# Routed blocks of 256 rows in place of pairs of 128-row tiles, in a transformer with routed experts

## The chip, the cores and the metric

The kernel runs on one core of a Trainium2 chip. The core has TensorE (PE in the profile, its weight loads PEld), VectorE (DVE), ScalarE (ACT), GpSimd (POOL) and SyncE (SP, which here only issues DMAs), SBUF as working memory and PSUM as the place where TensorE writes. The metric is the device time of one execution in microseconds: 3275.05 us, the median of 3 runs (3268.84 to 3275.7).

## The reference, cut to what matters

Sixteen sequences of 256 rows of 128 numbers pass a prologue (layer norm, a small wavelet network with linear attention) and then four layers of this:

```python
for l in range(4):
    h = rms(x, ln1_w[l])
    q, k, v = h @ wq[l], h @ wk[l], h @ wv[l]       # 16 query heads, 4 key/value heads of 64
    x = clip(x + attention(rope(q), rope(k), v, causal) @ wo[l], -100, 100)
    h = rms(x, ln2_w[l])
    probs = softmax(h @ wr[l])                      # 8 experts
    topv, topi = top_k(probs, 2)
    topv = topv / topv.sum(-1, keepdims=True)
    out = 0
    for e in range(8):                              # only rows that chose e count
        g = silu(h @ wg[l, e]) * (h @ wu[l, e])     # 128 -> 256
        out += comb[..., e:e+1] * (g @ wd[l, e])    # 256 -> 128
    x = clip(x + out, -100, 100)
```

Each row goes to two of eight experts. The kernel computes only those two per row.

## The kernel before

**The main loop.** `for it in range(-1, NIT + 1)` runs over 64 pairs of layer and sequence, and each engine has its own copy of this loop, written out by hand. One pass for `it` holds attention of sequence `it` (four groups `q` of four heads: `scores`, `mask_and_max`, `exps`, `normalise`, `attend`), the projections of `it + 1` (`project_qk`, `rope`) and output projection and routing of `it - 1` (`project_out`, `update_x`, `choose`, `route`). Each engine executes its instructions in order, and semaphores say when data or a PSUM bank is ready.

**The routed work.** `route` gives each row a slot in a region of its expert in HBM, and POOL sends the rows there by an indirect DMA (`scatter`, L1299). Eight sequences make a batch. When a batch is routed, `lay_out_tiles` (DVE) makes a table of tiles, 128 rows of one expert each; 40 tiles hold any distribution (32 full ones and up to 8 that are partly empty), and 40 are always computed, as 20 pairs. A pair takes two half-steps. In the even one `turn_rows` transposes 2 x 128 rows on PE (L891), `round_rows` (ACT, L1133) and `low_rows` (DVE, L1683) split them into a rounded part and a rest, and the pair before has its 4 gated blocks transposed (`turn_gated`, L912) and split (`round_gated` L1142, `low_gated` L1694). In the odd one `gate_and_up` multiplies each tile by its expert's weights, 3 products of 512 columns per tile (L902 to L904), ACT takes a tanh (`open_gate`, L1138), DVE two products (`gate`, L1689 and L1690), and the pair before goes through `down` (12 products of 128 columns, L926 to L928) and `copy_y` (ACT, L1147). SP fetches rows and weights and puts results back, two tiles separately: 8 DMAs a pair, each with a register load from the table (`tile_place`, L567).

**Where the half-steps stand.** A pass of the loop has eight places, 0 to 7, between its pieces. A batch's 42 half-steps are put in the next batch's passes: four in the second pass (places 4 to 7), all eight in the third to sixth, six in the seventh. The first and the eighth pass have none. I call a pass with all eight a dense pass: 4 pairs. The last batch has no later pass: its 42 half-steps run after the loop, the tail, with `finish` of the first eight sequences between them. Results come back by indirect DMAs (`gather`, L1275, in the loop and L1362 at the end).

**PSUM.** Eight banks form three rings. S (4 banks, freed by DVE): scores, q/k projections, output projection. T (2 banks, freed by ACT): transposed probabilities, v, h, logits, ranks, and y of the routed work. U (2 banks, freed by DVE): attention output, transposed rows, gates, transposed gated blocks. A tenant of a ring waits until the one that stood there before has been read.

## Time and profile before

| | |
|---|---|
| median of 3 runs | 3275.05 us |
| profiled execution, its own time | 3285.71 us |
| its span, first to last instruction | 3283.9 us |
| PE / PEld busy | 2618.0 us (80%) / 2095.5 us (64%) |
| DVE / ACT / POOL busy | 2207.6 (67%) / 1996.6 (61%) / 1861.3 us (57%) |
| granted TensorE clock, mean | 0.919 |
| DMA moved | 511.54 MB, of it 473.72 MB by SP's queue |

Busy shares are means over a prologue (to about 245 us), the loop (to about 3060 us) and the tail. A PE that is 80% busy is not at 80% of its peak: a matmul's time in the profile overlaps the next one's. For PE the distance between the starts of two neighbours says what one costs.

### The profile page before, as it was taken

The numbers are of one execution on the slowest core, as the hardware profiler recorded it, in microseconds if no ns is written. First come the engines' busy times: TensorE is split into PE (matmuls) and PEld (weight loads), VectorE is DVE, ScalarE is ACT, GpSimd is POOL, SyncE is SP. The second block draws the span as 40 slices with busy tenths as digits, with TensorE's granted clock in tenths as the row PEclk, the third lists the DMA queues.
The fourth block names the chain that finished last, engine by engine and source line by source line (L and its number), as shares of the span: only waits on it lengthen the run. The fifth ranks groups of instructions, "written<-read, shape, count | busy, mean of one in ns | idle before, by whom it ended". The sixth has DMA issues, their size and how long they took to land.

```text
span 3283.9 us, 66162 instructions
## 1 busy us (share of the span) xinstructions
PE 2618.0 (80%) x20406; PEld 2095.5 (64%) x20406; DVE 2207.6 (67%) x8164; ACT 1996.6 (61%) x7080; POOL 1861.3 (57%) x1662
## 2 busy tenths in 40 slices
PE   5317887898889987899789987898889978998572
PEld 2316666777667766777667766777677766776462
DVE  6686676666777667776676767677676666765343
ACT  3017677667667666666666766676666766666220
POOL 0026676545666667655765666566766576555403
PEclk9659999999999999999999999999999999999665
DMA  9211122556246642654256633654266624652574
GB/s 373 118 46 65 68 78 86 181 177 198 71 161 212 206 137 80 222 192 154 77 189 228 212 106 116 201 194 139 74 214 218 200 76 145 201 193 89 164 240 128
DMA packets 287022, 511.54 MB, mean 156 GB/s; under 512 B 39969, under 2 KB 159297, under 8 KB 286145
## 3 DMA queue, kind: packets, MB, share of 16 engines
q1 hardware_dynamic: 270288, 473.72, 42.6%
q0 software_dynamic: 16384, 33.59, 3.3%
q8 instruction: 167, 2.74, 0.4%
q14 instruction: 183, 1.49, 0.2%
HBM read 316.58 MB, written 106.69 MB: 129 GB/s over the span
## 4 chain that ended last, share of the span: by engine, by line
PE 43%; DVE 19%; ACT 12%; POOL 11%; issue 7%; SPq 3%; another core or an unknown queue 3%; DMA 2%; DVEq 0%; POOLq 0%
PE psum L784 6%; PE psum L802 6%; DVE arena L1572 5%; ACT arena L1055 4%; PE psum L759 4%; PE psum L852 4%; POOL arena L1308 4%; ACT arena L1063 3%; PE psum L804 3%; POOL arena L1275 2%; DVE arena L1593 2%; PE psum L902 2%; PE psum L832 2%; POOL rows_in L1299 2%
## 5 line engine op out<-in xcount | busy, mean ns | idle before, releaser
L1055 ACT ACTIVATE arena<-arena 128x128 f32<-128x128 f32 (+1 forms) x2048 | 902.3, 446 | 53.4 <-DVE arena L1597 47.5
L1308 POOL TENSOR_TENSOR arena<-arena 128x512 f32<-128x512 f32 (+1 forms) x512 | 743.6, 1472 | 208.4 <-DVE arena L1602 208.3
L1323 POOL TENSOR_TENSOR arena<-arena 128x512 f32<-128x512 f32 x320 | 401.6, 1282 | 491.6 <-DMA arena<-arena 491.3
L784 PE MATMUL psum<-arena 128*128 128x128 f32 x3072 | 478.1, 294 | 225.5 <-ACT arena L1063 154.9
L1063 ACT COPY arena<-psum 128x384 f32<-128x384 f32 x1024 | 447.5, 482 | 312.7 <-PE psum L784 217.4
L784 PEld LDWEIGHTS psum<-arena 128*128 128x128 f32 x3072 | 347.5, 147 | 341.0 <-ACT arena L1063 214.5
L759 PE MATMUL psum<-arena 64*128 64x128 f32 (+1 forms) x4096 | 419.8, 342 | 12.7 <-DVE arena L1593 7.0
L1593 DVE CUSTOM_DVE_ANT_0 arena<-psum,arena 128x256 f32<-128x256 f32 x1024 | 429.3, 419 | 0.0
L1606 DVE COPY arena<-psum 128x512 f32<-128x512 f32 x256 | 176.4, 689 | 347.3 <-PE psum L804 314.2
L1572 DVE TENSOR_TENSOR arena<-psum,arena 128x512 f32<-128x512 f32 x640 | 390.8, 675 | 1.9 <-PE psum L834 1.8
L1055 ACT ACTIVATION_READ_ACCUMULATOR arena<-arena 128x1 f32 x2048 | 389.9, 190 | 0.0
L802 PE MATMUL psum<-arena 128*64 128x256 f32 x2048 | 355.3, 428 | 35.7 <-DVE xT_lo L1683 30.2
L759 PEld LDWEIGHTS psum<-arena 64*128 64x128 f32 x4096 | 301.3, 190 | 55.7 <-issue 26.2
L1591 DVE CUSTOM_DVE_ANT_0 arena<-psum,arena 128x128 f32<-128x128 f32 x1024 | 292.4, 286 | 31.3 <-PE psum L759 17.0
L1299 POOL DMA_INDIRECT rows_in<-arena x256 | 259.4, 1013 | 75.3 <-issue 69.3
L852 PE MATMUL psum<-arena 128*128 128x128 f32 x2048 | 247.3, 279 | 27.6 <-issue 27.5
L852 PEld LDWEIGHTS psum<-arena 128*128 128x128 f32 x2048 | 240.3, 196 | 37.0 <-issue 36.5
L832 PE MATMUL psum<-h_hi,wqk_hi 128*128 128x256 f32 x640 | 197.1, 308 | 69.2 <-DVE arena L1593 52.6
L804 PEld LDWEIGHTS psum<-arena 128*64 128x64 f32 x2048 | 160.3, 150 | 91.6 <-issue 26.7
L1275 POOL DMA_INDIRECT arena<-rows_out,arena x192 | 189.1, 985 | 52.3 <-issue 52.3
L804 PE MATMUL psum<-arena 128*64 128x128 f32 x2048 | 215.1, 290 | 0.0
L1689 DVE SCALAR_TENSOR_TENSOR arena<-arena,psum 128x512 f32<-128x512 f32 x160 | 108.0, 675 | 149.2 <-ACT arena L1138 122.9
(199 smaller groups left out, 5440.5 us busy)
## 6 DMA issues: line engine op xcount, KB each, us to landing
gu<-gu_kept SPq DMA_DIRECT2D x320, 512.0 KB
wd<-wd_kept SPq DMA_DIRECT2D x320, 256.0 KB
arena<-arena SPq DMA_DIRECT2D x128, 384.0 KB, 3.0
arena<-arena SPq DMA_DIRECT2D x128, 256.0 KB
arena<-rows_in SPq DMA_DIRECT2D x320, 64.0 KB
rows_out<-arena SPq DMA_DIRECT2D x320, 64.0 KB
rows_in<-arena SPq DMA_DIRECT2D x34, 512.0 KB, 8.0
rows_out<-arena SPq DMA_DIRECT2D x34, 512.0 KB, 7.1
```

The source lines that it names most:

```text
L759: return T.matmul(psum[:, s_bank(("head", it, q, i)), cols], QKT[par][r, 2 + 2 * q + i // 2, rows * P:(rows + 1) * P], QKT[par][r, q // 2, ...
L784: mm = T.transpose(psum[:, t_bank(key), j * P:(j + 1) * P], probs[:, q, i, j * P:(j + 1) * P], ident)
L802: return T.matmul(psum[r, bank, c0:c0 + S], v[:, 0, kv], pt[:, 0:S], start=True, stop=False, skip_group_check=True)
L804: return T.matmul(psum[r, bank, c0 + P:c0 + S], v[:, 1, kv], pt[:, S:S + P], start=False, stop=True, skip_group_check=True)
L852: mm = T.matmul(psum[:, s_bank(("out", it)), t * P:(t + 1) * P], oT[:, c, t * P:(t + 1) * P], wo[:, c, :], start=(c == 0), stop=(c == NH / ...
L1055: ins = A.activation(a, a, ACT.Exp, bias=negmax[:, q, k:k + 1], accum_out=rowsum[:, q, k:k + 1])
L1063: A.copy(probsT[:, 4 * (q % 2) + i, :], psum[:, t_bank(key), 0:3 * P]).then_inc(sem("t_free"), 1)
L1299: G.indirect_dma_start(rows_in[b % 2], bass.IndirectOffsetOnAxis(place_of[:, it % B * ST + t, j:j + 1], 0), z2[:, it % 2, t, :], None).the ...
L1308: ins = G.tensor_tensor(a, a, r[:, :, t:t + 1].broadcast_to([P, 4, P * (t + 1)]), ALU.mult)
L1323: G.tensor_tensor(keys_and_queries(it, u), keys_and_queries(it, u), turned_part[:, u, :], ALU.add) \
L1572: return V.tensor_tensor(dst.rearrange("p (i s) -> p i s", i=2), psum[:, s_bank(("qk", it, u)), :].rearrange("p (i s) -> p i s", i=2), tab ...
L1593: V.tensor_tensor_reduce(probs[:, q, i, P:3 * P], psum[:, s_bank(key), P:3 * P], mask, SCALE, -3.0e38, ALU.add, ALU.max, rowmax[:, q, 2 * ...
```

## The change

**Blocks.** A unit of work is 256 rows of one expert instead of two tiles of 128. A batch of eight sequences needs 23 units for any distribution (16 + 7), one of four 15. Both halves of a unit use the same weights, so one fetch of 768 KB (`w_kept`, rounded part and rest of all three matrices) replaces two of 512 KB and two of 256 KB, and a unit has 3 DMAs instead of 8.

**Gates come out transposed.** `gate_and_up` has the weights as the stationary side and the rows as the moving one: 12 products of 256 columns instead of 6 of 512. Their result is already turned as `down` wants it, so `turn_gated` is gone, and `round_gated` and `low_gated` read SBUF.

**Rings.** Transposed rows move from the U ring to the T ring. ACT now writes them twice (rounded and exact), and DVE forms the rest from SBUF. Gates of units that run beside no scores (the last pass and the tail, the set `late`) use the S ring.

**Places.** A step is now `gate_and_up` of one unit, `turn_rows` of the next, `down` of the one before. A batch has 25 steps: places 5 and 7 of the second pass, places 1, 2, 3, 5, 7 of the third to sixth, 1, 2, 3 of the seventh. On ACT `round_gated` and on DVE `low_rows` and `low_gated` stand at the place's end, after the piece that follows.

**Batches.** The last batch of eight is cut in two of four. The first of these (15 units, 17 steps) stands at places 5 and 7 of the pass for `it` 62, 1 to 7 of 63 and 0 to 7 of 64; the second is the tail, with a third pair of HBM buffers.

```diff
-NB = NIT // HB
+FIRST = [HB * b for b in range(NIT // HB)] + [NIT - 4]
+END = FIRST[1:] + [NIT]
+NB = len(FIRST)
 CAP = HB * S
-PT = 20
-HS = 2 * PT + 2
-ROWS = NE * CAP + NE * P
+UR = 2 * P
+UNITS = [2 * (b - a) + NE - 1 for a, b in zip(FIRST, END)]
+UNIT0 = [sum(UNITS[:b]) for b in range(NB + 1)]
+ROWS = NE * CAP + NE * UR
...
+def step_places():
+    at = {}
+    for b in range(NB - 1):
+        last = END[b] - 1
+        if b < NB - 2:
+            places = [(last + 1 + u, p) for u, ps in ((1, (5, 7)), (2, (1, 2, 3, 5, 7)), (3, (1, 2, 3, 5, 7)),
+                                                      (4, (1, 2, 3, 5, 7)), (5, (1, 2, 3, 5, 7)), (6, (1, 2, 3))) for p in ps]
+        else:
+            places = [(NIT - 2, 5), (NIT - 2, 7)] + [(NIT - 1, p) for p in range(1, 8)] + [(NIT, p) for p in range(8)]
+        for k, where in enumerate(places):
+            at[where] = (b, k)
+    return at
...
+    def moe(b, k):
+        g = UNIT0[b] + k
+        if 1 <= k <= UNITS[b]:
+            ring = s if g - 1 in late else u
+            ring["gate", g - 1] = len(ring)
+            ring["up", g - 1] = len(ring)
+        if k < UNITS[b]:
+            t["rows", g] = len(t)
+        if k >= 2:
+            t["y", g - 2] = len(t)
...
+            def fetch(b, k):
+                g = UNIT0[b] + k
...
+                if g >= X_RING:
+                    t_is_full(sp, ("rows", g - X_RING))
+                if g >= W_RING:
+                    t_is_full(sp, ("y", g - W_RING))
+                sp.load([row_reg[g % ROW_REGS], expert_reg], tiles[k:k + 1, b % 2, :])
+                sp.dma_start(x_rows[:, g % X_RING, :, :], rows_in[buffer_of(b)][unit_rows(g), :].rearrange("(j p) c -> p j c", p=P)) \
+                    .then_inc(sem(f"x_rows_in{g % X_RING}"), 16)
...
+                sp.dma_start(w_now[:, g % W_RING, :, :].rearrange("p k n -> p (k n)").bitcast(F32), w_kept[which, :]) \
+                    .then_inc(sem(f"w_in{g % W_RING}"), 16)
...
+            def after_step(b, k):
+                if k >= 2:
+                    put_back(b, k - 2)
+                if 2 <= k < UNITS[b] - 2:
+                    fetch(b, k + 2)
+                if k == UNITS[b] + 1 and b == NB - 3:
+                    begin(b + 1)
...
             def gate_and_up(g):
-                pe.wait_ge(sem(f"gu_in{g % W_RING}"), 32 * (g // W_RING + 1))
-                u_was_read(pe, ("rows", g))
-                for j in range(2):
-                    key = ("gate", g, j)
-                    u_is_free(key)
-                    o = psum[:, u_bank(key), :]
-                    hi, lo = (a[:, j * P:(j + 1) * P] for a in (xT_hi, xT_lo))
-                    T.matmul(o, hi, gu[:, g % W_RING, j, 0:2 * FF], start=True, stop=False)
-                    T.matmul(o, hi, gu[:, g % W_RING, j, 2 * FF:4 * FF], start=False, stop=False)
-                    T.matmul(o, lo, gu[:, g % W_RING, j, 0:2 * FF], start=False, stop=True).then_inc(sem("u_full"), 1)
+                pe.wait_ge(sem(f"w_in{g % W_RING}"), 16 * (g // W_RING + 1))
+                pe.wait_ge(sem("xT_lo_ready"), g + 1)
+                hi, lo = (a[:, g % 2, :] for a in (xT_hi, xT_lo))
+                for m, name in enumerate(("gate", "up")):
+                    gate_is_free(name, g)
                     for f in range(2):
+                        o = psum[:, gate_bank(name, g), f * UR:(f + 1) * UR]
+                        w_h, w_l = (w_now[:, g % W_RING, k, (2 * m + f) * P:(2 * m + f + 1) * P] for k in range(2))
+                        T.matmul(o, w_h, hi, start=True, stop=False)
+                        T.matmul(o, w_h, lo, start=False, stop=False)
+                        mm = T.matmul(o, w_l, hi, start=False, stop=True)
+                    mm.then_inc(gate_full(g), 1)
...
+            def step_of(b, k):          # TensorE
+                g = UNIT0[b] + k
+                if 1 <= k <= UNITS[b]:
+                    gate_and_up(g - 1)
+                if k < UNITS[b]:
+                    turn_rows(g)
+                if k >= 2:
+                    down(g - 2)
...
             def round_rows(g):
-                u_is_full(act, ("rows", g))
-                A.mul(xT_hi, psum[:, u_bank(("rows", g)), 0:2 * P], lnw[:, 1, l:l + 1]).then_inc(sem("xT_hi_ready"), 1)
+                t_is_full(act, ("rows", g))
+                rows = psum[:, t_bank(("rows", g)), 0:UR]
+                A.mul(xT_hi[:, g % 2, :], rows, lnw[:, 1, l:l + 1])
+                A.mul(xT[:, g % 2, :], rows, lnw[:, 1, l:l + 1]).then_inc(sem("t_free"), 1)
...
             def round_gated(g):
-                u_is_full(act, ("gated", g))
-                A.copy(hh_hi, psum[:, u_bank(("gated", g)), :]).then_inc(sem("hh_hi_ready"), 1)
+                gate_was_read(act, "up", g)
+                A.copy(hh_hi, gated).then_inc(sem("hh_hi_ready"), 1)
...
             def low_gated(g):
                 dve.wait_ge(sem("hh_hi_ready"), g + 1)
-                V.tensor_tensor(hh_lo, psum[:, u_bank(("gated", g)), :], hh_hi.bitcast(F32), ALU.subtract) \
-                    .then_inc(sem("u_free"), 1)
+                V.tensor_tensor(hh_lo, gated, hh_hi.bitcast(F32), ALU.subtract).then_inc(sem("hh_lo_ready"), 1)
...
-            for hs in range(HS):
-                moe(NB - 1, hs)
-                if hs % 4 == 3 and hs // 4 < HB:
-                    finish(hs // 4)
+            for k in range(UNITS[-1] + 2):
+                step_of(NB - 1, k)
+                step_end(NB - 1, k)
+                if k % 2 == 0 and 1 <= k // 2 <= HB:
+                    finish(k // 2 - 1)
```

The order of instructions moves on every engine. TensorE at place 2 of a dense pass, before: `project_v` (L841), the rows and gated blocks turned (L891, L912), `project_out` (L852).

```order
L841 MATMUL psum<-arena 128x256 [waits t_free,wv_in]
L841 MATMUL psum<-arena 128x256
L891 MATMUL psum<-arena 128x128 [waits u_free,x_rows_in1]
L891 MATMUL psum<-arena 128x128
L912 MATMUL psum<-arena 128x128 [waits u_free]
L912 MATMUL psum<-arena 128x128 x3
L852 MATMUL psum<-arena 128x128 [waits s_free,u_free,wo_in]
```

The same place now: `project_v` (L861), `gate_and_up` (L929 to L931), `turn_rows` (L911), `down` (L942 to L944), `project_out` (L872).

```order
L861 MATMUL psum<-arena 128x256
L929 MATMUL psum<-xT_hi,w_now 128x256 [waits u_free,xT_lo_ready,w_in0]
L930 MATMUL psum<-xT_lo,w_now 128x256
L931 MATMUL psum<-xT_hi,w_now 128x256
...
L929 MATMUL psum<-xT_hi,w_now 128x256 [waits u_free]
...
L911 MATMUL psum<-arena 128x128 [waits t_free,x_rows_in1]
L911 MATMUL psum<-arena 128x128
L942 MATMUL psum<-w_now,hh_hi 128x128 [waits t_free,hh_lo_ready]
...
L872 MATMUL psum<-arena 128x128 [waits s_free,u_free,wo_in]
```

Six transposes ahead of `project_out` have become a whole step of 26 products, and two of its waits are now for the T ring, whose tenants here run v, rows, y.

ScalarE at place 1 of a dense pass, before: tanh (L1138), `copy_y` (L1147), the copies of probabilities (L1063), squares of the coming sequence (L1077).

```order
L1138 ACTIVATE arena<-psum 128x512 [waits u_full]
L1147 ACTIVATE arena<-psum 128x256 [waits y_rows_out0,t_full]
L1063 COPY arena<-psum 128x384 [waits t_full] x4
L1077 ACTIVATE arena<-arena 128x128 [waits x_ready]
L1077 ACTIVATE arena<-arena 128x128
```

The same place now: tanh (L1154), rows rounded and copied (L1149, L1150), `copy_y` (L1164), the probabilities (L1074), `round_gated` (L1159), the squares (L1088).

```order
L1154 ACTIVATE arena<-psum 128x512 [waits u_full]
L1149 ACTIVATE xT_hi<-psum,arena 128x256 [waits t_full]
L1150 ACTIVATE arena<-psum,arena 128x256
L1164 ACTIVATE arena<-psum 128x256 [waits y_rows_out0,t_full]
L1074 COPY arena<-psum 128x384 [waits t_full] x4
L1159 CAST hh_hi<-arena 128x512 [waits u_free]
L1088 ACTIVATE arena<-arena 128x128 [waits x_ready]
L1088 ACTIVATE arena<-arena 128x128
```

Two instructions at this place have become five, one of them behind the probabilities and ahead of the squares.

## Rows read from the trace of the kernel before

**Rows 1.** The page's chain of waits that ended last, shares of the span by engine.

```profile
PE 43%; DVE 19%; ACT 12%; POOL 11%; issue 7%; SPq 3%; another core or an unknown queue 3%; DMA 2%; DVEq 0%; POOLq 0%
```

**Rows 2.** Stretches: us, busy PE, PEld, DVE, ACT, POOL, PEclk, DMA share, GB/s.

```profile
1337.00:1525.00 188.00, 171.55 (x1400) 140.56 (x1396) 133.20 (x516) 129.40 (x458) 111.44 (x100) 0.99 0.60 200
3043.00:3067.00 24.00, 9.55 (x83) 7.62 (x79) 6.97 (x38) 4.14 (x14) 9.84 (x12) 0.78 0.06 23
3067.00:3236.00 169.00, 117.70 (x480) 97.57 (x480) 67.78 (x136) 40.29 (x80) 29.71 (x32) 0.63 0.72 231
```

**Rows 3.** L1612, once a pass: count, first and last start, in three windows.

```profile
L1612 DVE TENSOR_TENSOR arena<-arena,psum x5: 420/421/422, 368.2 to 512.7; 128x256 f32<-128x256 f32 x5
...
L1612 DVE TENSOR_TENSOR arena<-arena,psum x4: 410/410/420, 1357.6 to 1499.4; 128x256 f32<-128x256 f32 x4
...
L1612 DVE TENSOR_TENSOR arena<-arena,psum x9: 410/420/422, 1357.6 to 1713.8; 128x256 f32<-128x256 f32 x9
```

**Rows 4.** Instructions by line in the four dense passes: busy, mean ns, idle before.

```profile
L802 PE MATMUL psum<-arena 128*64 128x256 f32 x128 | 21.1, 408 | 5.4 <-DVE xT_lo L1683 4.1 <-ACT arena L1063 1.2
...
L1694 DVE TENSOR_TENSOR hh_lo<-psum,hh_hi 128x512 fp32r<-128x512 f32 x16 | 10.9, 681 | 0.0
L1689 DVE SCALAR_TENSOR_TENSOR arena<-arena,psum 128x512 f32<-128x512 f32 x16 | 10.8, 672 | 9.1 <-ACT arena L1138 7.7 <-issue 1.4
...
L1138 ACT ACTIVATE arena<-psum 128x512 f32<-128x512 f32 x16 | 9.4, 585 | 6.3 <-PE psum L904 6.3
L1142 ACT CAST hh_hi<-psum 128x512 fp32r<-128x512 f32 x16 | 9.3, 584 | 0.0
...
L1133 ACT ACTIVATE xT_hi<-psum,arena 128x256 fp32r<-128x256 f32 x16 | 7.5, 472 | 4.5 <-PE psum L891 4.5
...
L1683 DVE SCALAR_TENSOR_TENSOR xT_lo<-psum,arena,xT_hi 128x256 fp32r<-128x256 f32 x16 | 7.3, 454 | 14.3 <-ACT xT_hi L1133 14.3
...
L1147 ACT ACTIVATE arena<-psum 128x256 f32<-128x256 f32 x16 | 6.0, 375 | 1.6 <-PE psum L928 1.4 <-issue 0.2
```

**Rows 5.** Timeline of PE in one dense pass: start us, us, what.

```profile
1399.71 0.38 PE L891 MATMUL psum<-arena 128*128 128x128 f32 x2
...
1400.37 3.74 PE L852 MATMUL psum<-arena 128*128 128x128 f32 x32
...
1405.82 0.50 PE L902 MATMUL psum<-gu,xT_hi 128*128 128x512 f32 x1
...
1407.31 0.22 PE L926 MATMUL psum<-wd,hh_hi 128*128 128x128 f32 x1
...
1408.60 0.33 PE L832 MATMUL psum<-h_hi,wqk_hi 128*128 128x256 f32 x1
...
1410.08 0.38 PE L861 MATMUL psum<-arena 128*128 128x128 f32 x2
```

**Rows 6.** Timeline of DVE and of ACT, same pass.

```profile
1398.86 0.69 DVE L1606 COPY arena<-psum 128x512 f32<-128x512 f32 x1 [1.56 <-PE psum L804]
...
1401.88 0.56 ACT L1067 COPY arena<-psum 128x512 f32<-128x512 f32 x1
```

**Rows 7.** Timeline of PE in the tail.

```profile
3075.26 0.80 PE L902 MATMUL psum<-gu,xT_hi 128*128 128x512 f32 x1 [1.29 <-DMA gu<-gu_kept]
...
3137.54 0.76 PE L902 MATMUL psum<-gu,xT_hi 128*128 128x512 f32 x1 [1.30 <-issue]
...
3142.72 0.66 PE L891 MATMUL psum<-arena 128*128 128x128 f32 x2
```

**Rows 8.** Chain of waits in the tail: start us, us, what.

```profile
3064.88 2.22 DMA rows_in<-arena
...
3221.62 0.77 PE psum L902
...
3236.11 0.94 POOL arena L1362
...
3275.16 2.54 DMA arena<-rows_out,arena
```

404 lines of the change are left out of this document (185 added, 219 removed).

## The prediction

> **What bounds the kernel now.** I read the page first. Its chain of waits [rows 1] passes through PE for 43% of the span, DVE 19%, ACT 12%, POOL 11%: PE leads, but no engine alone sets the time. Then the spacing of one instruction that stands once in each pass, the add of `update_x` [rows 3]. Without routed work (368.2 to 512.7, four distances) a pass takes 36.1 us, a dense one (1357.6 to 1499.4, three distances) 47.3, and eight passes of a batch 356.2 (1357.6 to 1713.8), of which the four that are not dense keep 167.0, or 41.7 each. Four pairs thus add 11.2 us. Third, the stretch of four dense passes [rows 2]: in 188 us PE is busy 171.55, DVE 133.20, ACT 129.40. Per pass PE has 4.1 us without work, ACT 14.7 and DVE 13.7, and the clock is granted at 0.99, the level of 2.4 GHz. The tail is another regime: clock 0.63, mostly at 1.2 GHz, DMA at 231 GB/s, and a pair takes (3221.62 - 3075.26) / 19 = 7.70 us [rows 7, 8].
>
> **The change in a dense pass.** PE's work I take from distances between starts [rows 5]. A pair costs 0.66 for six transposes (1399.71 to 1400.37), 1.49 for two tiles of gates (1405.82 to 1407.31) and 1.29 for `down` (to 1408.60), together 3.44. A unit has 2 of the 6 transposes, 0.22, the same `down`, 1.29, and 12 products of 256 columns. These have the shape of `project_qk`, of which 12 took 1.48 (1408.60 to 1410.08). That makes 2.99. A batch costs PE 20 x 3.44 = 68.8 before and 23 x 2.99 = 68.8 now: the padding of 23 blocks eats exactly what the transposes gave. But the five places put 5 x 2.99 = 14.95 in a dense pass that had 4 x 3.44 = 13.76: +1.2.
>
> ACT [rows 4]: a pair has 0.472 + 0.585 + 0.584 + 0.375 = 2.02, a unit one more copy of the rows (0.472), 2.49. Five against four: 12.4 - 8.1 = +4.4 a pass. DVE: 0.454 + 2 x 0.672 + 0.681 = 2.48 for either (`low_rows` and `low_gated` now read SBUF; I keep their PSUM prices), so +2.5. Both fit in the idle time of 14.7 and 13.7 by sum, not necessarily by place.
>
> `round_gated` reads SBUF instead of PSUM; the nearest row is its present form, 584 ns [rows 4]. The Trainium skill (VectorE: DVE Perf Modes, The TRN2 errata) gives ScalarE a fixed 224 cycles for an SBUF source and 172 for PSUM, at 1.2 GHz, so an estimate from that page is 613 against 570 ns for 512 columns. The trace's 584 is near the second. By the page ACT gets 191 x 0.04 = 8 us more over the kernel, by the row nothing; both are off the path of my sum.
>
> Waits of PE. One goes: attention's second product (L802) waited 4.1 us in four passes for `low_rows` to free a U bank [rows 4], 1.0 a pass. Transposed rows no longer stand in that ring. One comes, at place 2. PE is through with `project_v` at 1399.71 [rows 5]. The gates there want `low_rows` of the step before, which on DVE now stands behind the copy of attention's output (1398.86 + 0.69 = 1399.55 [rows 6]) and takes 0.45: 1400.0, and with a hand-over 1400.1, a wait of 0.4. Gates and transposes take 1.70, so `down` is reached at 1401.8. Its bank in the T ring held v, and v is read at 1401.88 + 0.56 = 1402.44 [rows 6], because on ACT that copy stands behind eight exponentials. Another 0.6. Queued behind `down` is `project_out`, then h, the scores and, through `update_x`, everything of the second half. (v's copy itself moves by -0.66, the transposes gone from place 0, and +0.58, `round_gated` now ahead of the squares: nothing.) So +1.2 - 1.0 + 1.0 = +1.2. I take +1.5, as some of ACT's 4.4 will be in the way. Bounds: all of ACT's extra on the path, +4.4; or eight hand-over points made five take 3/8 of PE's 4.1 idle, -1.5, and the place-2 wait does not come: 1.2 - 1.0 - 1.5 = -1.3.
>
> The other passes have 5 pairs and now 5 units, PE -2.2, against one place-2 wait in the seventh: -1.0 a batch (-2.2 to +2). **Loop:** 7 x (4 x 1.5 - 1.0) = **+35** (-52 to +137).
>
> I give nothing for the weights' traffic, 1.5 MB a pair down to 0.75 a unit. No idle time in rows 4 ends on it; what hides it is the lead of the fetches, and if that were too short the tail would tell first. The prologue zeroes half as many HBM buffers again; by the slices of the page DMA stands still there while VectorE works on the wavelets, so 0.
>
> **Passes 62 to 64.** They take 17 steps of the first half-batch. The pass for 62 goes from three pairs to five units, from 41.7 to 48.8: +7. The one for 63 had nothing and gets 7 units, 20.9 us of PE. At the dense rate (11.2 us for 13.76 of work) that is +17; if they fill all of the 10 us that a light pass leaves PE, +11. It has no projections for a coming sequence, so 12. The last pass, 3043 to 3067, is a chain of latencies with PE busy for 9.55 of 24 us [rows 2]. Eight units are 23.9 us of PE and 14.4 are free: +9.5 at best, +24 at worst; every step also wants its answer from ACT and DVE, so 14. Together **+33** (27 to 48).
>
> **The tail.** Rows have landed at 3064.88 + 2.22 = 3067.10, gates run from 3075.26 to 3221.62, the last results are back when POOL gathers at 3236.11, and 31 distances to 3275.16 make 1.26 us a gather [rows 7, 8]. The span ends at 3283.9, 216.8 us after the rows landed. Now there are 15 units. At the low clock a pair without transposes took 5.18 (3137.54 to 3142.72 [rows 7]) where 1.49 + 1.29 = 2.78 stood in the loop, a factor of 1.86; a unit's 2.99 becomes 5.6. I take 5.7, PE setting the pace. SP's part falls from 8 DMAs to 3, and 1.05 MB in 5.7 us is 184 GB/s, below the 231 reached. So 8.2 to the first gate, 14 x 5.7 = 80 to the last, 14.5 to the gather, and only four sequences wait for it: 47.8 - 16 x 1.26 = 27.6. That is 130: **-87**. Bounds: 14 x 7.70 if the pace stays, -59; 14 x 4.5 if the clock rises and the hand-over loop binds (half of the gates 0.74, tanh 0.59, two products 1.34, `low_rows` 0.45, and `finish` every second step, 1.2), -103.
>
> **Sum:** 35 + 33 - 87 = -19. The profiled execution took 3285.7 (1.8 more than its span), 10.7 above the median of 3275.05, so 3267 for it and **3256** for the median.
>
> **Rivals.**
> *A: fewer hand-overs win.* A dense pass falls by 1.3. For: PE's idle time is made of short waits, and the tenants that blocked attention leave the U ring; DVE waited 14.3 us in four passes for rounded rows (L1683) [rows 4], a wait that now has slack. Against: PE, already busy 91%, gets more work. 7 x (-5.2 - 1.0) = -43, the total -97: 3178.
> *B: slower.* At places 1 and 2 the path is ACT, DVE, ACT, not PE. At place 1 ACT gets both copies of the rows and `round_gated`, less tanh and `copy_y` that were there: +1.5. At place 2 `update_x` stands behind tanh, two products of DVE, `round_gated` and `low_gated`, where it stood behind one rounding and two subtractions: +2.0. If neither is covered a pass costs +3.5, the loop 7 x 13 = +91, the total +37: 3312. It decides from a loop of +54, a dense pass of +2.2. For: ACT is without a pause from place 1 to 2 but for waits for PE. Against: PE reaches `update_x` later by its own step.
> *C: the clock rises in the tail.* PE stands idle there between steps and is granted 0.63 [rows 2]. Now its steps would follow each other closely, as in the dense passes that have 0.99. 14 x (5.7 - 4.5) = -17: 3239. The Trainium skill (TensorE: Matmul & The Clock Gate, Why this matters for your kernels) says that matmuls without gaps keep the full clock and that a wait for DMA in each turn loses it. By that rule C is the case, by the row the low clock stays, since PE was busy 117.70 of 169 us there and did not get it.
> *D: the tail's pace stays at 7.7*, by DMA latency or order: +28, 3284, no change.
>
> **Chances.** Forecast 0.36 (3225 to 3290 by itself), A 0.22, B 0.24, C 0.12, D 0.06. Within 0.2%, 3268.5 to 3281.6, is what measuring this kernel can't tell from no change. Faster: 0.75 of the forecast, all of A, 0.9 of C, 0.3 of D = 0.62, rounded down to 0.61; slower: B nearly whole, a tenth of the forecast: 0.28; same 0.11. The range of 3180 to 3325 takes in A's value less a little, B's, and leaves out a loop near its bounds.
>
> **What would show it.** Right: products of 256 columns 0.12 us apart in the loop; `update_x` every 48.8 us in dense passes; PE idle before `down` at place 2, ended by ACT's copy of v; about 130 us from the landing of the last rows to the end, units 5.7 apart; 16 gathers after the last result. Wrong: dense passes at 46 or at 51 us (A, B); a granted clock above 0.8 in the tail (C); units 7.7 apart (D); or a wait for weights, which no term holds.

## The result: slower by 1.4%, and the profile after

The changed kernel takes 3315.0 us (3311.2 to 3321.6), the kernel before beside it 3275.4 (3268.8 to 3286.7): a ratio of 1.014, 95% interval 1.0112 to 1.0169. Forecast was 3256. Run again on two more chips the ratio was 1.0194 [1.0168, 1.0220] and 1.0206 [1.0177, 1.0235]: slower each time, but by amounts that differ more than their intervals, so a comparison with the changed kernel is safe only between kernels that ran on one chip. The profiled execution has a span of 3309.4 us, 25.5 more than before.

The page of the changed kernel, where the engines' busy time, the clock, DMA and the chain of waits stand:

```profile
PE 2637.2 (80%) x21532; PEld 2153.6 (65%) x21532; DVE 2365.2 (71%) x8304; ACT 2115.2 (64%) x7395; POOL 1888.1 (57%) x1662
...
PEclk9659999999999999999999999999999999999876
...
DMA packets 230644, 439.13 MB, mean 133 GB/s; under 512 B 28273, under 2 KB 155281, under 8 KB 229777
...
PE 38%; DVE 22%; ACT 17%; POOL 13%; issue 7%; DMA 2%; another core or an unknown queue 1%; SPq 0%; DVEq 0%; POOLq 0%; ACTq 0%
```

Beside [rows 1], PE's part of the chain fell from 43% to 38%, and DVE and ACT together went from 31% to 39%. The clock in the tail is up, and DMA moved 439 MB for 512 before.

The add of `update_x`, once a pass (L1623, L1612 before): count, duration in ns, first and last start in three windows. The second fence is the kernel before in the last of these windows.

```profile
L1623 DVE TENSOR_TENSOR arena<-arena,psum x4: 420/420/422, 1371.9 to 1522.3; 128x256 f32<-128x256 f32 x4
...
L1623 DVE TENSOR_TENSOR arena<-arena,psum x5: 420/422/422, 363.8 to 508.2; 128x256 f32<-128x256 f32 x5
...
L1623 DVE TENSOR_TENSOR arena<-arena,psum x3: 414/420/420, 3042.2 to 3156.6; 128x256 f32<-128x256 f32 x3
```

```profile
L1612 DVE TENSOR_TENSOR arena<-arena,psum x3: 420/422/422, 2980.7 to 3052.3; 128x256 f32<-128x256 f32 x3
```

A pass without routed work is as before [rows 3]: (508.2 - 363.8) / 4 = 36.1. A dense one takes (1522.3 - 1371.9) / 3 = 50.1 for 47.3. At the third-last update the changed kernel is 3042.2 - 2980.7 = 61.5 us late, at the last one 3156.6 - 3052.3 = 104.3.

Stretches of the changed kernel (us, busy PE, PEld, DVE, ACT, POOL, clock, DMA share, GB/s): three dense passes between updates, then pass 62, pass 63 to the last update, and the tail.

```profile
1371.95:1522.28 150.33, 135.73 (x1157) 113.99 (x1155) 111.41 (x399) 108.13 (x372) 85.92 (x75) 1.00 0.43 142
3042.00:3094.00 52.00, 42.03 (x336) 34.34 (x335) 32.14 (x122) 31.40 (x110) 23.19 (x19) 0.90 0.39 132
3094.00:3157.00 63.00, 51.09 (x401) 44.72 (x401) 32.31 (x95) 34.61 (x98) 14.11 (x12) 0.92 0.51 171
3157.00:3282.00 125.00, 79.39 (x512) 76.19 (x510) 73.52 (x183) 46.10 (x104) 52.14 (x55) 0.75 0.57 178
```

Against [rows 2], PE's busy time per dense pass rose from 42.9 to 45.2 and its idle time from 4.1 to 4.9.

Lines in four dense passes of the changed kernel (busy us, mean ns, idle before and what ended it), which answer to [rows 4]:

```profile
L929 PE MATMUL psum<-xT_hi,w_now 128*128 128x256 f32 x80 | 25.2, 315 | 2.2 <-DVE arena L1617 1.7
L942 PE MATMUL psum<-w_now,hh_hi 128*128 128x128 f32 x80 | 22.5, 281 | 3.7 <-ACT arena L1078 3.7
L822 PE MATMUL psum<-arena 128*64 128x256 f32 x128 | 20.2, 393 | 0.1
L1710 DVE TENSOR_TENSOR hh_lo<-arena,hh_hi 128x512 fp32r<-128x512 f32 x20 | 18.2, 909 | 1.7 <-ACT hh_hi L1159 1.7
...
L1702 DVE SCALAR_TENSOR_TENSOR arena<-arena,psum 128x512 f32<-128x512 f32 x20 | 13.5, 676 | 19.5 <-ACT arena L1154 19.3
L1159 ACT CAST hh_hi<-arena 128x512 fp32r<-128x512 f32 x20 | 12.3, 615 | 7.0 <-DVE arena L1706 7.0
...
L1694 DVE TENSOR_TENSOR xT_lo<-arena,xT_hi 128x256 fp32r<-128x256 f32 x19 | 7.7, 407 | 0.0
```

Attention's product (L822, L802 before) no longer waits for `xT_lo`. `down` (L942) waits for the copy of v, 3.7 us in four passes. `round_gated` (L1159) takes 615 ns and not 584. And `low_gated` (L1710) has a mean of 909 ns where it had 681 with a PSUM source. Over the whole kernel it ranges from 677 to 2385:

```profile
L1710 DVE TENSOR_TENSOR hh_lo<-arena,hh_hi x191: 677/692/2385, 611.8 to 3273.6; 128x512 fp32r<-128x512 f32 x191
```

### The profile page after: what moved, and what is told of

Read it like the earlier page. It is cut to its first block, busy times and chain, and to the rows that moved or that the text cites. A ratio compares the mean times of both kernels' runs of the same rounds, so it can differ in the third digit from the quotient of the medians.

```text
span 3309.4 us, 65991 instructions
## 1 busy us (share of the span) xinstructions
PE 2637.2 (80%) x21532; PEld 2153.6 (65%) x21532; DVE 2365.2 (71%) x8304; ACT 2115.2 (64%) x7395; POOL 1888.1 (57%) x1662
## 4 chain that ended last, share of the span: by engine, by line
PE 38%; DVE 22%; ACT 17%; POOL 13%; issue 7%; DMA 2%; another core or an unknown queue 1%; SPq 0%; DVEq 0%; POOLq 0%; ACTq 0%
PE psum L804 7%; ACT arena L1066 7%; PE psum L872 5%; PE psum L822 5%; POOL arena L1320 4%; ACT arena L1074 3%; POOL arena L1287 3%; DVE arena L1604 3%; DVE arena L1583 2%; POOL rows_in L1311 2%; PE psum L779 2%; PE psum L824 2%; PE psum L929 2%; DVE arena L1602 2%; PE psum L852 2%
## 5 line engine op out<-in xcount | busy, mean ns | idle before, releaser
L1320 POOL TENSOR_TENSOR arena<-arena 128x512 f32<-128x512 f32 (+1 forms) x512 | 769.3, 1522 | 281.9 <-DVE arena L1613 281.9
L804 PE MATMUL psum<-arena 128*128 128x128 f32 x3072 | 486.4, 294 | 240.6 <-ACT arena L1074 145.1
L1074 ACT COPY arena<-psum 128x384 f32<-128x384 f32 x1024 | 449.4, 479 | 296.1 <-PE psum L804 248.9
L1335 POOL TENSOR_TENSOR arena<-arena 128x512 f32<-128x512 f32 x320 | 402.2, 1283 | 407.2 <-DMA arena<-arena 407.1
L779 PE MATMUL psum<-arena 64*128 64x256 f32 (+1 forms) x4096 | 423.6, 343 | 19.0 <-POOL arena L1335 10.5
L822 PE MATMUL psum<-arena 128*64 128x256 f32 x2048 | 349.6, 422 | 3.3 <-ACT arena L1074 3.2
L929 PE MATMUL psum<-xT_hi,w_now 128*128 128x256 f32 x764 | 246.5, 323 | 51.6 <-issue 40.4
L872 PE MATMUL psum<-arena 128*128 128x128 f32 x2048 | 249.2, 280 | 23.6 <-issue 23.6
L852 PE MATMUL psum<-h_hi,wqk_hi 128*128 128x256 f32 x640 | 195.9, 306 | 85.3 <-DVE arena L1604 78.8
L872 PEld LDWEIGHTS psum<-arena 128*128 128x128 f32 x2048 | 240.3, 196 | 32.5 <-issue 32.4
L1702 DVE SCALAR_TENSOR_TENSOR arena<-arena,psum 128x512 f32<-128x512 f32 x191 | 129.5, 678 | 171.0 <-ACT arena L1154 157.5
L942 PE MATMUL psum<-w_now,hh_hi 128*128 128x128 f32 x764 | 218.7, 286 | 30.1 <-ACT arena L1078 22.2
L931 PE MATMUL psum<-xT_hi,w_now 128*128 128x256 f32 x764 | 222.1, 291 | 0.0
```

The lines of the kernel that those rows point to most:

```text
L779: return T.matmul(psum[:, s_bank(("head", it, q, i)), cols], QKT[par][r, 2 + 2 * q + i // 2, rows * P:(rows + 1) * P], QKT[par][r, q // 2, ...
L804: mm = T.transpose(psum[:, t_bank(key), j * P:(j + 1) * P], probs[:, q, i, j * P:(j + 1) * P], ident)
L822: return T.matmul(psum[r, bank, c0:c0 + S], v[:, 0, kv], pt[:, 0:S], start=True, stop=False, skip_group_check=True)
L872: mm = T.matmul(psum[:, s_bank(("out", it)), t * P:(t + 1) * P], oT[:, c, t * P:(t + 1) * P], wo[:, c, :], start=(c == 0), stop=(c == NH / ...
L1074: A.copy(probsT[:, 4 * (q % 2) + i, :], psum[:, t_bank(key), 0:3 * P]).then_inc(sem("t_free"), 1)
L1320: ins = G.tensor_tensor(a, a, r[:, :, t:t + 1].broadcast_to([P, 4, P * (t + 1)]), ALU.mult)
```

## The experiments

All edit the changed kernel, and their line numbers differ by a few from its own. A dense pass is the spacing of `update_x` unless said otherwise. "After the first mask" counts from the instruction that closes the first `mask_and_max` of a pass (L1608), as a mean over all 28 dense passes.

### First round: one wait, one resource, one part

**`copy_o` ahead of the last two ropes** (DVE).

```
 place(it, 6)
+if now: copy_o(it, 1)
 if coming: rope(it + 1, range(N_QK1, N_QK))
 place_end(it, 6)
-if now: copy_o(it, 1)
```

> The changed kernel with one exchange on VectorE: in every pass the copy of attention's second output (copy_o of group 1) stands ahead of the last two ropes instead of behind them. In the changed kernel's dense passes TensorE waits about 1.5 us at place 7 for that copy, because the up half of the gates wants its bank. Theory W (the time was lost in new waits for ring banks): the wait goes, about 1.2 us of 28 dense and some other passes come back, 25 to 40 us faster than the changed kernel. Theory P (VectorE is stretched beside GpSimd) and theory N (the passes are filled by the work of 23 units instead of 20 pairs): the wait only moves, within 10 us of the changed kernel.

Measured: 3422.3 us, ratio 1.0424 [1.0406, 1.0442]. Far slower, and no theory had it. Ropes 3 and 4 came 2.8 us later in a pass (45.1 us after the first mask; 42.3 in the run with one last batch below, which has the changed kernel's dense passes and ran on this chip), and what follows them (the turning DMA, GpSimd's adds and normalising) stands behind them. That this is what cost the time is argued from the order of work, not tested. Its chain of waits at place 1 to 2 also shows what DVE's `low_gated` can do (start us, us, what):

```profile
1464.54 0.81 DVE xT_lo L1694
1465.35 2.32 DVE hh_lo L1710
...
1467.71 0.33 PE psum L942
```

**v copied between the exponentials ahead of place 2** (ACT).

```
-exps(it, 1); copy_v(it)
+exps(it, 1, range(2)); copy_v(it); exps(it, 1, range(2, 4))
```

> The changed kernel with ScalarE's copy of v put between the two halves of group 1's exponentials, 1.8 us earlier. It tests the wait that the prediction named at place 2, 0.6 us forecast and about 1.2 us in the trace, of down for the bank that held v. Theory W: the wait goes and 28 to 35 passes gain about 1 us, 25 to 40 us in all. Theories P and N: ScalarE then gives the exponentials and the reciprocal later and nothing is gained, within 10 us.

Measured: 3328.3, ratio 1.0123 [1.0103, 1.0143]. The changed kernel did not run on this chip; what the edit gave is read below, against the run with one last batch.

**`low_gated` on 128 of its 512 columns** (the rest of that product's low half is left out).

> The changed kernel with low_gated on VectorE cut to 128 of its 512 columns (the rest of the low part stays zero: left out of the computation). In the changed kernel this instruction takes 0.69 us, but 1.5 to 2.4 us in 49 of 191 cases, 183 us in all; cut it should take 0.29 us and 0.7 or so where stretched. Theory P: VectorE's time on the way to the bank's release is what lengthened the passes, so 40 to 70 us faster than the changed kernel. Theory W alone: the place 7 wait shrinks by the time taken from VectorE ahead of the copy, 15 to 30 us. Theory N: under 15 us.

Measured: 3319.6, ratio 1.0108 [1.0091, 1.0125]. I first read this as the end of the theory that this instruction matters. The trace says otherwise: the cut did not remove the wait it was to remove. DVE, then GpSimd beside it:

```profile
1412.47 1.98 DVE L1710 TENSOR_TENSOR hh_lo<-arena,hh_hi 128x128 fp32r<-128x128 f32 x1
```

```profile
1411.23 3.08 POOL L1320 TENSOR_TENSOR arena<-arena 128x512 f32<-128x512 f32 x2
```

Alone it takes 0.28 us; beside GpSimd 1.98, against 2.39 in full width, and 55 of 191 still took over 1 us. So only the instruction's own part shrank; the rest is a wait.

**The last eight sequences as one batch** (FIRST without `NIT - 4`; 23 units in the tail).

> The changed kernel with the last eight sequences in one batch of 23 units after the loop, as the kernel before has them in 20 pairs; all else as changed. The split added 54 us between the last dense pass and the landing of the last rows. Without it those come back but the tail has 8 more units at 5.6 us and four more sequences to gather, 45 + 20 us: so 5 to 20 us slower than the changed kernel. If the split's steps were dearer than the tail they save, it is faster by 10 or more.

Measured: 3348.0, ratio 1.0203 [1.0186, 1.0221]. Up to the update of pass 61 this kernel and the changed one run almost the same code (the changed one has 15 more small instructions on DVE, for the table of the half-batch), so the rest can be read apart:

```profile
L1621 DVE TENSOR_TENSOR arena<-arena,psum x3: 420/420/422, 3075.3 to 3143.8; 128x256 f32<-128x256 f32 x3
```

From 3075.3 to its span's end at 3335.9 it takes 260.6 us, the changed kernel 3309.4 - 3042.2 = 267.2, and 269.1 and 268.7 in its two later traces. The split of the last batch thus gains nothing, and may cost 7 us; the difference in the whole time was the chip's loop. I had expected the split to be worth 5 to 20 us. The same reading makes this run a control for its neighbours, on the same chip: the loop ended at 3075.3 here, at 3058.9 with v copied early and at 3060.2 with the narrow `low_gated`, so each gave some 15 us, and at 3153.6 with `copy_o` first. This is from one execution each, and the one here is the quickest of its kernel's four by 9 us. For v copied early that is more than theories P and N allow and less than W wanted; for the narrow `low_gated` it lies where N's range ends and W's begins, far from P's 40 to 70.

### Second round: where the step of place 2 might stand

**Place 2 to place 4, and to place 0** (tables of `step_places`).

```
-(2, (1, 2, 3, 5, 7)) ... (6, (1, 2, 3))
+(2, (1, 3, 4, 5, 7)) ... (6, (0, 1, 3))      first kernel
+(2, (0, 1, 3, 5, 7)) ... (6, (0, 1, 3))      second kernel
```

> The same 25 steps of a batch, with the step of place 2 moved to place 4 in the dense passes (places 1, 3, 4, 5, 7; in the last pass of a batch 0, 1, 3). Theory M (the loss sits before project_out: the whole step at place 2 stands ahead of it on PE and ahead of update_x on DVE, and update_x came 3.8 us later in a pass): update_x goes back to about 19 us after the first mask (22.7 in the changed kernel), the idle of PE before down that the copy of v ended goes, a dense pass falls from 50.5 to about 48.5, the four of a batch give 8 us and the loop 50 to 60: ratio about 0.998. Theory N (five steps of 2.5 us of ACT and of DVE are too much work for a pass wherever they stand): what place 2 gives back is lost at place 4, where attention's product and the copy of its output wait behind the step; a pass stays within 0.5 us of 50.5 and the ratio within 0.005 of 1.014.

> The same 25 steps, the step of place 2 moved to place 0 (0, 1, 3, 5, 7 in the dense passes; 0, 1, 3 in the last). Theory M: update_x stands at about 19 to 20 us again, the dense pass at 48.5 to 49.5, ratio 1.000 to 1.006. Theory N: the path at places 0 and 1 (masks, the copies of the probabilities on ACT, exponentials) takes the whole step instead, mask 1 and all behind it come 2 to 3 us later, a pass at 50 to 51.5, ratio 1.01 to 1.02.

Measured: 3394.3, ratio 1.0602 [1.0554, 1.0649], and 3379.8, ratio 1.0548 [1.0495, 1.0602], both far worse than either theory said. In the first, `update_x` came 15.4 us after the first mask and not 22.7, earlier even than theory M wanted; then PE stood at place 4:

```profile
1449.04 3.67 DVE L1583 TENSOR_TENSOR arena<-psum,arena 128x512 f32<-128x512 f32 x6
1452.63 0.41 DVE L1694 TENSOR_TENSOR xT_lo<-arena,xT_hi 128x256 fp32r<-128x256 f32 x1
```

```profile
1453.14 0.40 PE L929 MATMUL psum<-xT_hi,w_now 128*128 128x256 f32 x1 [2.79 <-issue]
```

The gates of place 4 want `low_rows` of the step at place 3, which on DVE stands behind six rope products. That is 2.79 us of PE, and attention's product, queued behind, waits too. The clock adds to it: the twelve products behind this pause start 0.21 us apart, the lower of the two levels, where they are 0.12 apart elsewhere in the loop. With place 0 it is the step of place 7 before it, whose `low_rows` stands behind the masks: PE waits 2.39. In both traces, then, two steps in a row found DVE taken between them.

**The gated product left in PSUM** (the product writes the up bank; `round_gated` and `low_gated` read it; one counter for each bank of the U ring).

```
-V.tensor_tensor(flat(gated), flat(opened), psum[:, gate_bank("up", g), :], ALU.mult).then_inc(gate_free(g), 1)
+up = psum[:, gate_bank("up", g), :]
+V.tensor_tensor(up, flat(opened), up, ALU.mult).then_inc(sem("gated_ready"), 1)
...
-V.tensor_tensor(hh_lo, gated, hh_hi.bitcast(F32), ALU.subtract)...
+V.tensor_tensor(flat(hh_lo), psum[:, gate_bank("up", g), :], flat(hh_hi).bitcast(F32), ALU.subtract)...
```

> The gated product is left in its PSUM bank and low_gated and round_gated read it there, so low_gated has one SBUF input as in the kernel before; each bank of the U ring gets a counter of its own. The up bank comes free some 1.5 us later. Theory P (the stretched low_gated, 49 of 191 at 1.4 to 2.4 us beside GpSimd, sum 51 us, is on the path): low_gated flat at about 680 ns, dense pass 50.0, kernel 5 to 20 us faster than the changed one, ratio 1.008 to 1.012. Rival (the later release costs more than the stretch): the wait of attention's second product for a U bank comes back, 1 to 2 us a pass, ratio 1.018 to 1.03.

Measured: 3235.8 where before was 3200.3, ratio 1.0108 [1.0071, 1.0146]. `low_gated` is flat (mean 684 ns, none of 191 over 1 us), and beside the changed kernel's 1.014 the ratio is what theory P wanted; but that one is from another chip. Its dense passes, 47.9 us with the clock at 1.00:

```profile
1349.69:1493.43 143.74, 134.44 (x1157) 113.49 (x1155) 108.30 (x399) 108.31 (x372) 83.50 (x75) 1.00 0.46 150
```

This chip ran the kernel before 2.3% faster, so the price is better read from a later pair on one chip (below): 26 us.

**20 of a batch's 23 units** (three are left out), steps at 1, 3, 5, 7.

> Each batch of eight sequences computes 20 units and leaves three of its 23 out; four steps in a dense pass, at places 1, 3, 5, 7, and four in the last pass. It says what the fifth step costs. By PE's work, 2.99 less a pass: 47.5. Theory M: the fifth step costs more than its own PE time since it is the one at place 2: a dense pass of 46.5 to 47.2, below the 47.9 of the kernel before, which had the same PE work of four pairs and more; the loop loses 28 x 3.5 = 98 us and the ratio is 0.98 to 0.985. Theory N, in which any step costs: about 48 to 48.5, ratio 0.988 to 0.995.

Measured: ratio 0.9954 [0.9930, 0.9978]. Dense passes of 43.3 us, but 54.2 for the pass with a step at place 0. The ratio is at the upper end of theory N's and far from M's. The fourth round has 20 units without a step at place 0.

### Third round: on one chip with the changed kernel

> The changed kernel unchanged, on this chip, so that passes of the other kernels of this run are compared on one chip. Ratio 1.014 within its interval, 1.011 to 1.017; dense passes of 49 to 51 us. If the ratio stands elsewhere, differences between kernels of different chips may not be read to a per cent.

Measured: 3348.5, ratio 1.0194 [1.0168, 1.0220], outside the 1.011 to 1.017 that I expected.

**The step of place 2 behind `project_out`** (PE), `update_x` (DVE) and the copy of h (ACT). PE's part of the edit; the other engines move the place in the same way:

```
-place(it, 2)
 if old: project_out(it - 1)
 if coming: turn_h(it + 1)
+place(it, 2)
```

> The step of place 2 is moved on every engine behind project_out and the transposes of h (PE), update_x and low_h (VectorE), the squares and the copy of h (ScalarE); nothing else is changed. Theory M (what matters is that the step stands ahead of project_out and update_x): update_x 18 to 19 us after the first mask, dense pass 49 or less, ratio 1.000 to 1.008. Theory N' (a fifth step costs 6 to 7 us since PE has no more than 2 us idle in a pass of four steps, 43.5, and each step brings its 3 to 3.7 us and one more wait, wherever it is): 49.5 to 51 and a ratio of 1.010 to 1.018.

Measured: 3315.6, ratio 1.0107 [1.0076, 1.0137], 33 us under the changed kernel beside it. `update_x` stands 18.1 us behind the first mask for 23.3, and the mean distance of first masks in all dense passes falls from 51.3 to 49.6. The place of `update_x` is theory M's; the pass and the ratio are inside what N' gave, though the gain, 0.9%, is of M's size once the changed kernel stands at 1.0194. So the place of this step counts, and it is not all: the fifth step costs elsewhere too. The edit also takes v's bank out of `down`'s way, so it does not tell the step's own work from that wait.

**25 steps spread three, five, four, five, four, four** (pass 1 at 4, 5, 7; pass 6 at 1, 3, 4, 5).

> The 25 steps of a batch spread otherwise: pass 1 has three (4, 5, 7), passes 2 and 4 five (1, 2, 3, 5, 7), passes 3 and 5 four (1, 3, 5, 7), pass 6 four (1, 3, 4, 5), for the first six batches. Theory F (a pass of four steps at 1, 3, 5, 7 costs 43.5, one of five 50, as the run with 20 units and the changed kernel show): two passes a batch give 6.5 each, passes 1 and 6 take back 2 each: 9 us a batch, 54 over six, ratio 0.996 to 1.000. Rival L (20 units were fast since less work was there in all; the work has to be done somewhere): the cycle of eight passes stays at 365 to 368, ratio 1.010 to 1.016.

Measured: 3352.3, ratio 1.0222 [1.0188, 1.0255]: no gain, as rival L had it. Four-step passes fell to 46.0 and 46.5, but the pass with steps at 1, 3, 4 and 5, one step more than it had, paid it back: 10.8 us longer than in the changed kernel.

**The same with the gated product in PSUM.**

> The spread of the run before (three, five, four, five, four, four) together with the gated product left in its PSUM bank, which alone gave a ratio of 1.011 against 1.014. If both gains add: 0.992 to 0.997, faster than either kernel. If they are one gain (the same wait): as the run before within 0.002.

Measured: 3326.0, ratio 1.0130 [1.0104, 1.0156]. Against its neighbour on this chip, 3352.3 - 3326.0 = 26 us. In that neighbour 64 of 191 `low_gated` took over 1 us, 74 us above 0.69 each in sum, so a third of this came back. The edit also gives `round_gated` a PSUM source (some 0.03 us each, off the path) and each U bank its own counter, so the 26 us are the price of the whole edit; that `low_gated` is its main part is argued.

### Fourth round: the price of a fifth step, and both mends

> The kernel before, unchanged, for its trace on this chip: passes of the runs beside it are then compared on one chip. Dense passes 47 to 48.5 us (47.9 in its first trace), ratio 1.

> Each batch of eight sequences computes 20 units and leaves three of its 23 out, as in the earlier run with 20 units, but the last pass of a batch keeps places 1, 2, 3 and the first gets 4, 5, 7, so that no step stands at place 0: what is left is the price of the fifth step alone. Theory F: the dense passes of four steps take 43 to 44 us, 4 less than the kernel before on this chip (fewer hand-overs: four steps of a whole block for eight half-steps), the cycle of eight passes 340 to 345, ratio 0.975 to 0.985. Rival (four steps were only that fast since the pass before or behind them took the wait): dense 46 to 47, ratio as before, 0.993 to 0.998.

Measured: 3133.9, ratio 0.9759 [0.9717, 0.9801], and this chip's trace of the kernel before (one execution, 3205.0 us). Three dense passes each, the kernel before and then 20 units:

```profile
1323.45:1458.79 135.34, 127.93 (x1057) 105.28 (x1057) 99.45 (x388) 97.87 (x345) 83.55 (x76) 1.00 0.61 205
```

```profile
1313.08:1441.99 128.91, 123.41 (x1077) 104.27 (x1077) 102.68 (x387) 101.75 (x358) 85.69 (x76) 1.00 0.42 142
```

That is 45.1 us with four pairs (47 to 48.5 was expected of this kernel; the chip is a quick one) and 43.0 with four units: -2.1, and -1.5 as a mean over all 28 dense passes, first mask to first mask (45.1 and 43.6). The prediction's own prices, 4 x 2.99 for 4 x 3.44, give -1.8 of PE's work, and the wait of attention's product that goes, another -1.0. So blocks at four places gain about what PE's work said and no more: nothing is seen of a gain from fewer hand-overs.

**Both mends** (place 2 behind `update_x`, gated product in PSUM).

> The step of place 2 behind project_out and update_x (alone 1.0107 where the changed kernel had 1.0194), and the gated product left in its PSUM bank (alone 1.0108 where the changed kernel had 1.014 to 1.019). If the two gains add: 1.000 to 1.005. If both shorten the same wait at place 2: 1.007 to 1.011. Dense passes 47 to 49.

Measured: 3202.9, ratio 0.9990 [0.9964, 1.0017]. 1.000 to 1.005 was expected if the two gains add, so they do, as far as ratios of different chips can be set side by side, and the loss is gone. Its dense passes, 46.8 us:

```profile
1329.92:1470.25 140.33, 132.97 (x1155) 113.47 (x1155) 108.57 (x400) 107.77 (x373) 83.79 (x76) 1.00 0.46 153
```

Against the run with 20 units, a fifth step costs 46.8 - 43.0 = 3.8 us here, with 2.99 of PE's products in it. (The two kernels also differ in the two mends. Inside the run with 25 steps spread, first mask to first mask, passes of five steps take 51.2 and those of four 47.3: 3.9.)

**Both, and steps spread three, five, four, five, five, three** for the first six batches.

```
+PLACES = ((1, (4, 5, 7)), (2, (1, 2, 3, 5, 7)), (3, (1, 3, 5, 7)), (4, (1, 2, 3, 5, 7)), (5, (1, 2, 3, 5, 7)), (6, (1, 2, 3)))
```

> The two edits of the run before, and the 25 steps of the first six batches spread three, five, four, five, five, three (the first pass 4, 5, 7, the third dense one 1, 3, 5, 7). Theory F: a pass of four steps saves 6 us, the step in the first pass costs 2, so 4 us a batch or 24 in all below the run before: 0.993 to 0.998, faster than both kernels. Rival L (what a pass saves comes back in the next one): equal to the run before within 0.002.

Measured: 3197.7, ratio 0.9967 [0.9948, 0.9987]. That is 5 us under the run before, not 24, and the two intervals overlap, so the new spread by itself is not shown to gain.

> The changed kernel unchanged, beside the best version, once more: ratio 1.014 to 1.020 as in its two other comparisons. A fifth step costs what its dense pass is above 43.4 us on a quick chip, or above 45 to 46 on a slow one.

> The best version unchanged (step behind update_x, gated product in PSUM, three, five, four, five, five, three), on what may be another chip. If its gain holds: ratio 0.994 to 0.999. If it was the quick chip's alone: 1.000 to 1.005.

Measured on another chip: the changed kernel 3350.3, ratio 1.0206 [1.0177, 1.0235]; the best version 3279.8, ratio 0.9993 [0.9976, 1.0010]. It beats the changed kernel by 2% there. Against the kernel before it is 0.3% faster on one chip and the same on the other. The changed kernel's and the best version's dense passes on that chip:

```profile
1383.58:1536.99 153.41, 138.62 (x1149) 116.94 (x1146) 112.44 (x399) 108.19 (x372) 85.95 (x75) 0.97 0.43 141
```

```profile
1353.95:1497.45 143.50, 131.49 (x1129) 111.64 (x1129) 106.41 (x395) 105.41 (x368) 84.22 (x76) 0.99 0.43 142
```

51.1 and 47.8 us a pass, the latter with one four-step pass of three. The changed kernel's clock is 0.97 here where its first trace has 1.00; why is not shown.

## Why the prediction was wrong, step by step

**The sum.** Forecast 35 + 33 - 87 = -19. In the spans of the two traces it was +61.5, +53.8 and -89.8: +25.5. Two terms failed: the loop's, through the price of a dense pass, and the one for passes 62 to 64. The first alone, 26 us too low, turns the sign. (In medians the change costs 39.6 us and not 25.5: the traced execution of the kernel before lies 10.7 us above its median, that of the changed kernel 3.8 below. What is read from this pair of traces is therefore rather too little.)

**The tail: right in sum, and not for the reason given.** Rows landed, the first gate, and the gather that waits for the last result in the chain of the changed kernel:

```profile
3180.15 2.21 DMA rows_in<-arena
...
3189.39 0.58 PE psum L929
...
3281.25 1.20 POOL arena L1373
```

```profile
L929 PE MATMUL psum<-xT_hi,w_now x60: 280/415/583, 3189.4 to 3269.3; 128*128 128x256 f32 x60
```

From 3182.4 to the end are 127.0 us where 130 were forecast; the last unit's gates start at 3267.3, so 14 distances of 5.56 (forecast 5.7). Rival D (7.7) is out. Of C the clock half came (0.75 in this stretch, 0.63 in [rows 2]), but not the pace of 4.5 that went with it. PE early in the tail, behind its longest pause, and late; one line stands for every third product of 256 columns:

```profile
3194.62 0.28 PE L929 MATMUL psum<-xT_hi,w_now 128*128 128x256 f32 x1
3194.98 0.28 PE L929 MATMUL psum<-xT_hi,w_now 128*128 128x256 f32 x1
...
3205.26 0.56 PE L929 MATMUL psum<-xT_hi,w_now 128*128 128x256 f32 x1 [7.88 <-issue]
...
3268.00 0.41 PE L929 MATMUL psum<-xT_hi,w_now 128*128 128x256 f32 x1
3268.64 0.41 PE L929 MATMUL psum<-xT_hi,w_now 128*128 128x256 f32 x1
```

Three products take 0.36 us at the high level of the clock and 0.64 at the low one, and the two change places through the whole tail: the first unit ran at the low level, the second at the high one, the third, behind the pause of 7.88 us, at the low one again. I had PE set the pace at the low level, 2.99 x 1.86. In the trace it does not: from 3189.4 to 3270.0 PE is idle for 22.8 of 80.6 us, nearly all of it before gates that start 0.1 us after DVE's `low_rows` has ended. What sets the pace is this exchange between PE, ACT and DVE, C's "hand-over loop", at another length than C gave it. One of the 14 distances, with the long pause, is 11.1 us, and the other 13 have a mean of 5.1. That 5.56 fell so near 5.7 is luck, and the cause of the long pause is not shown.

One question was never put: is the split of the last batch needed for this gain? By the run with one last batch it is not. There everything from pass 62 on took 260.6 us, in the changed kernel 267.2, before 3283.9 - 2980.7 = 303.2. The gain came with the blocks and not with the split.

**The loop: the dense pass was mis-sized, +1.5 forecast, +2.9 measured.** From first mask to first mask the 28 dense passes take 50.6 us in mean for 47.8, in all 80 us more for a forecast of 42; the rest of the way to the third-last update gave back 18.5, for 7. "Products of 256 columns 0.12 us apart" held, and so did the price of a unit. Three things did not.

*First, place 2.* The waits were there, and in sum as forecast. What was wrong is how they and the step's work count. PE, then ACT, in one dense pass:

```profile
1463.37 0.36 PE L929 MATMUL psum<-xT_hi,w_now 128*128 128x256 f32 x1
...
1464.87 0.38 PE L911 MATMUL psum<-arena 128*128 128x128 f32 x2
1466.49 0.30 PE L942 MATMUL psum<-w_now,hh_hi 128*128 128x128 f32 x1 [1.23 <-ACT arena L1078]
...
1467.85 3.79 PE L872 MATMUL psum<-arena 128*128 128x128 f32 x32
```

```profile
1465.77 0.57 ACT L1078 COPY arena<-psum 128x512 f32<-128x512 f32 x1
...
1466.83 0.59 ACT L1154 ACTIVATE arena<-psum 128x512 f32<-128x512 f32 x1
```

Here `down` waits 1.23 us for v's bank; as a mean over the 28 dense passes PE stands idle 0.91 us before `down` and 0.18 before these gates, 1.1 together, where I had 0.6 and 0.4. With its own work the step puts 4.2 us ahead of `project_out` in mean (4.5 in this pass), in place of 0.66 of transposes, and `update_x` comes 22.7 us after the first mask for 18.8. The wrong thought was to add this step's extra at place 2 and take off the pairs' at the other places, as if PE's time were one sum over the pass. Place 2 stands on the path to `update_x`, h and the scores: of the 3.9 us only 1.1 came back by the end of the pass. Moving the step behind `update_x`, and with it `down` away from v's bank, gave 1.7 us a pass and 33 us in all.

*Second, a price that rows of before could not show.* "I keep their PSUM prices" was the sentence. DVE and GpSimd of the changed kernel:

```profile
1439.68 0.41 DVE L1694 TENSOR_TENSOR xT_lo<-arena,xT_hi 128x256 fp32r<-128x256 f32 x1
1440.01 1.76 DVE L1710 TENSOR_TENSOR hh_lo<-arena,hh_hi 128x512 fp32r<-128x512 f32 x1
...
1441.80 2.43 DVE L1583 TENSOR_TENSOR arena<-psum,arena 128x512 f32<-128x512 f32 x4
```

```profile
1437.20 4.02 POOL L1335 TENSOR_TENSOR arena<-arena 128x512 f32<-128x512 f32 x3 [7.58 <-DMA arena<-arena]
```

Of the 191 `low_gated` 49 took over 1 us, 51 us in sum above 0.69 each, and every one of them started beside one of GpSimd's adds of 512 columns (L1320, L1335) and ended 0.55 us after that add did, whatever the add still had to run (0.9 to 1.8 us). The 118 that met no such instruction took 691 ns (median). The other 24 started beside an add of two columns (L1295, 0.72 us in the trace, 0.4 of it gone) and took 0.68 to 0.69, so not every GpSimd instruction holds one up. Behind `low_gated` in DVE's order stand the two ropes, `copy_o` and, waiting for its bank, the gates of place 7: PE idle for 1.47 us at 1444.88, another wait that I had not listed. In this pass the chain of waits runs through the 1.68 us of that instruction. Reading PSUM instead (with what that edit brings along) gave 26 us. The Trainium skill (SBUF — State Buffer, SBUF: two separate sides) says that a VectorE instruction with two SBUF inputs and a GpSimd instruction that reads SBUF share a port pair which the first of them locks until it is done. The traces agree for the 49, and with the narrow `low_gated`, which ends 0.15 us after GpSimd's add and not 0.55, they tell it from a slower rate. That rule spoke against this very edit, and the prediction did not weigh it.

*Third, `round_gated`*: 615 ns, as the estimate from the Trainium skill (VectorE: DVE Perf Modes, The TRN2 errata) had it (613), not the row's 584. That is 6 us of ACT over the kernel and, as said, off the path.

**Passes 62 to 64: +53.8 for +33, beyond the bound of 48.** Pass 62 took 51.9 for 38.3 (+13.6, forecast 7), pass 63 62.5 for 33.3 (+29.2, forecast 12), and the last stretch +11.0 (14). In pass 62 two more steps at the 3.9 us that a fifth step costs in the loop would be 8, and the other 6 have no cause on record. In pass 63 seven steps were priced at 20.9 us of PE less 9 of the pass's idle time, and that is the step that failed: PE's busy time rose from 25.0 to 50.6 us, and its idle time did not shrink but grew, from 8.3 to 11.9. Of the 11.9, 9.7 stand before the gates of six steps, and each of these waits ended 0.1 us after DVE's `low_rows` of the same rows. One of them, DVE and then PE:

```profile
3131.31 0.37 DVE L1694 TENSOR_TENSOR xT_lo<-arena,xT_hi 128x256 fp32r<-128x256 f32 x1
```

```profile
3131.79 0.55 PE L929 MATMUL psum<-xT_hi,w_now 128*128 128x256 f32 x1 [2.79 <-issue]
```

At neighbouring places a step's rows are not ready in time, as in the two runs with the step moved to place 4 or 0.

**The rivals.** *A*: a dense pass of four steps is indeed 1.5 to 2.1 us shorter, but by PE's own work; it is the fifth step that turns the sign. *B*: its number (3312) was met, its mechanism half, and the number by luck: its loop was +91 for 61.5 in the traces, and the 21 us that passes 62 to 64 cost beyond the forecast fill most of the gap. The extra at places 1 and 2 is the right place and size (+2.2 was the turning point, +2.9 came). But it named DVE's queue ahead of `update_x`; the rows show `update_x` waiting for PE, and PE for ACT's copy. I had written against B that "PE reaches `update_x` later by its own step": that was the cause itself, and not an argument against it.

## What to carry to other kernels

Price a step by where it stands: time put ahead of the instruction that the rest of a pass hangs on counts nearly in full, and time saved behind it counts in part (here 1.1 of 3.9 us came back). Where an edit turns a PSUM operand into an SBUF one, look at what GpSimd does at that moment before keeping the old price. And check that an experiment which shrinks an instruction shrinks the part that is in question: here a quarter of the columns left the wait whole.
